# One-core sparse spike FFN: batch 0's chain moved into the wait for batch 1's totals, the idle row made ahead of the last table chunks, and all stores but one held behind the second gather of w1 rows

## The reference, cut to what matters

```python
# x: (2, 2048, 512) float32, cond: (2, 512), w1: (512, 2048), w2: (2048, 512)
rates = relu(x) * 0.001
c = cond[:, None, :] + cumsum(rates, axis=1)          # along the 2048 tokens
fl = floor(c)
prev = concatenate([floor(cond)[:, None, :], fl[:, :-1, :]], axis=1)
spikes = (fl - prev) / 0.001
h = relu(spikes @ w1 + b1)
out = x + h @ w2 + b2
```

## Time and profile before

| what | us |
|---|---|
| median of three runs | 105.44 (105.04 to 106.31) |
| the profiled execution's own time | 105.28 |
| its span in the profile | 103.4 |
| last store issued by SP | 81.32 |
| first scatter of batch 1 on POOL | 91.21 |
| last scatter (general rows) on POOL | 98.68 |
| last matmul of the general FFN ends | 96.37 |

### The profile page before, as it was taken

How to read it: one execution, slowest core, us unless ns; L and a number is a source line. 1 busy time by engine, 2 the same in 40 slices (tenths; PEclk the granted TensorE clock), 3 DMA queues, 4 the chain that set the end, 5 groups by cost and what they waited for, 6 DMA issues and landing times.

```text
span 103.4 us, 1080 instructions
## 1 busy us (share of the span) xinstructions
PE 90.7 (88%) x325; PEld 46.2 (45%) x325; DVE 67.9 (66%) x152; ACT 36.5 (35%) x66; POOL 34.3 (33%) x39
## 2 busy tenths in 40 slices
PE   5999999999999999999999699992699999999200
PEld 5934444444644444644132235440656666665000
DVE  3448999989599999485848758998999500012200
ACT  2886515415281540569940000002136222222000
POOL 6220000000068600017604894000000678568840
PEclk9999999999999999999999999999759999999995
DMA  2999999999999999940000069989999999968770
GB/s 78 287 375 396 421 420 412 406 406 410 415 407 411 378 401 398 411 184 6 10 3 0 0 222 412 282 257 409 418 437 421 424 437 361 205 157 87 102 130 30
DMA packets 8203, 29.55 MB, mean 286 GB/s; under 512 B 1639, under 2 KB 1767, under 8 KB 6914
## 3 DMA queue, kind: packets, MB, share of 16 engines
q1 hardware_dynamic: 6192, 25.43, 61.9%
q0 software_dynamic: 1856, 4.00, 18.0%
q10 hardware_dynamic: 146, 0.01, 0.1%
HBM read 19.48 MB, written 10.75 MB: 292 GB/s over the span
## 4 chain that ended last, share of the span: by engine, by line
PE 44%; DVE 25%; DMA 9%; ACT 7%; issue 4%; POOL 4%; POOLq 2%; DVEq 0%
PE ps_table L886 37%; DVE x_sb L748 15%; DMA out<-x_sb 9%; POOL out L379 4%; PE ps_small L1017 4%; ACT w_sb L456 3%; ACT w_sb L455 2%; POOLq L55 2%; PE ps_turn L923 2%; DVE place_hot L693 1%; PE ps_idle L912 1%; DVE under L611 1%; DVE place_slot L700 1%; ACT block_sum L465 1%; ACT idle_base L486 0%
## 5 line engine op out<-in xcount | busy, mean ns | idle before, releaser
L886 PE MATMUL ps_table<-w_sb 128*128 128x512 f32 x128 | 58.5, 603 | 0.0
L886 PEld LDWEIGHTS ps_table<-w_sb 128*128 128x128 f32 x128 | 23.4, 192 | 24.2 <-issue 23.1
L368 POOL DMA_INDIRECT rates<-in_x_turned,sixteen_at x8 | 9.8, 1225 | 35.5 <-DVE sixteen_at L615 33.7
L379 POOL DMA_INDIRECT out<-w_sb,to_single x8 | 12.5, 1565 | 20.0 <-DMA out<-x_sb 18.2
L455 ACT ACTIVATE w_sb<-w_sb,b_col 128x512 f32<-128x512 f32 (+2 forms) x19 | 12.2, 643 | 17.0 <-DMA w_sb<-in_w_pairs 16.9
L601 DVE SCALAR_TENSOR_TENSOR total_two<-x_sb,total_two 128x1024 f32<-128x1024 f32 x14 | 17.1, 1225 | 0.8 <-DMA x_sb<-in_x 0.4
L991 PE MATMUL ps_table<-w_sb 128*128 128x512 f32 x32 | 17.2, 626 | 0.0
L748 DVE TENSOR_TENSOR x_sb<-x_sb,ps_idle 128x2048 f32<-128x2048 f32 x7 | 15.6, 2281 | 0.1
L456 ACT ACTIVATE w_sb<-w_sb,minus_relu_b 128x512 f32<-128x512 f32 (+2 forms) x19 | 12.3, 649 | 0.6
L983 PEld LDWEIGHTS ps_turn<-place_slot,w_sb 128*128 128x128 f32 x32 | 5.2, 209 | 7.6 <-issue 7.0
L559 DVE SCALAR_TENSOR_TENSOR idle_part<-w_sb,relu_b,idle_part 128x512 f32<-128x512 f32 x9 | 6.8, 753 | 1.7 <-DMA w_sb<-in_w_pairs 1.5
(11 more groups left out here) (152 smaller groups left out, 61.7 us busy)
## 6 DMA issues: line engine op xcount, KB each, us to landing
x_sb<-in_x SPq DMA_DIRECT2D x16, 512.0 KB, 14.5
out<-x_sb SPq DMA_DIRECT2D x8, 1024.0 KB, 8.1
w_sb<-in_w_pairs SPq DMA_DIRECT2D x15, 512.0 KB, 15.6
w_sb<-in_w_pairs SPq DMA_DIRECT2D x2, 256.0 KB, 2.9
b_row<-in_b SPq DMA_DIRECT2D x1, 256.0 KB, 15.5
rates<-in_x_turned,sixteen_at POOLq DMA_INDIRECT x8, 4.3
out<-w_sb,to_single POOLq DMA_INDIRECT x8, 5.7
w_sb<-in_w,w_at POOLq DMA_INDIRECT x2, 8.0
```

What stands on the lines that cost most here:

```text
L368: pool.indirect_dma_start(out=rates[:, col, :], out_offset=None, in_=x_sixteen, in_offset=bass.IndirectOffsetOnAxis(ap=sixteen_at[:, col:c ...
L379: pool.indirect_dma_start(out=out_rows, out_offset=bass.IndirectOffsetOnAxis(ap=to, axis=0), in_=row, in_offset=None, bounds_check=last_ro ...
L886: last = pe.matmul(ps_table[c][:, :], table_hidden[:, m, c * P:(c + 1) * P], w2_sb[:, m, :], start=(m == 0), stop=(m == FC - 1))
```

## The change

What it does:

- PE takes one more chunk of the idle row and DVE one less (`BY_HAND` 9 becomes 8).
- SP's second store (batch 0, tokens 4 to 7) first waits for `w1_got[1]`, the landing of the second gather of w1 rows. The six stores behind it on SP wait with it.
- POOL issues the first gather of w1 rows ahead of its adds, no longer waits for `places_ready` before them, and adds 8 tokens of batch 0 instead of 4: seven between the two gathers, one behind the second. DVE adds the other 8 tokens of batch 0: one behind `find_tokens(1)`, one behind `number_general(1)`, two and four behind `list_places(1)`.
- DVE runs `find_tokens(0)` ahead of `find_blocks(1)`, and the rest of batch 0's chain up to `list_places(0)` ahead of `find_tokens(1)`.
- PE turns batch 0's blocks behind chunk 6, and takes batch 0's steps and the strips earlier among the table's parts.
- ACT copies batch 0's turned blocks behind chunk 10, and the two idle copies and batch 1's turned blocks ahead of chunks 14 and 15.

```diff
--- before.py
+++ after.py
@@ -37,7 +37,7 @@
     WQ = 4
     STRIP = 32
     STRIPS = P // STRIP
-    BY_HAND = 9
+    BY_HAND = 8
     WARM = 8
     FAR = 4.0 * ROWS
     NEVER = 1.0e30
@@ -326,6 +326,8 @@
                 sp.dma_start(out_blk[b, :, piece(q), :], x_sb[b][:, piece(q), :]).then_inc(idle_stored[b], 16)
 
             for b, q in ((0, 0), (0, 1), (0, 2), (0, 3), (1, 0), (1, 1), (1, 2), (1, 3)):
+                if (b, q) == (0, 1):
+                    sp.wait_ge(w1_got[B - 1], 16)
                 store_idle(b, q)
             for b in range(B):
                 sp.wait_ge(idle_stored[b], 16 * XQ)
@@ -389,12 +391,11 @@
 
             get_sixteens(0)
             get_sixteens(1)
+            get_w1(0)
             pool.wait_ge(idle_copied, 1)
-            pool.wait_ge(places_ready, 1)
-            add_idle(0, 0, 2)
-            get_w1(0)
-            add_idle(0, 2, 4)
+            add_idle(0, 0, 7)
             get_w1(1)
+            add_idle(0, 7, 8)
             pool.wait_ge(singles_listed, 1)
             for b in range(B):
                 if b == 1:
@@ -480,13 +481,14 @@
                     copy_sums(0)
                 if m == 11:
                     copy_sums(1)
-                if m == 14:
+                if m == 10:
                     copy_blocks(0)
-            act.wait_ge(strips_summed, 1)
-            act.activation(idle_base[:, :], ps_idle[:, :], ACT.Copy).then_inc(strips_copied, 1)
-            act.wait_ge(idle_summed, 1)
-            act.activation(idle_row[:, :], ps_idle[:, :], ACT.Copy).then_inc(idle_copied, 1)
-            copy_blocks(1)
+                if m == 13:
+                    act.wait_ge(strips_summed, 1)
+                    act.activation(idle_base[:, :], ps_idle[:, :], ACT.Copy).then_inc(strips_copied, 1)
+                    copy_blocks(1)
+                    act.wait_ge(idle_summed, 1)
+                    act.activation(idle_row[:, :], ps_idle[:, :], ACT.Copy).then_inc(idle_copied, 1)
 
             def relu_hidden(m, summed, count, ready):
                 act.wait_ge(summed, count)
@@ -748,6 +750,8 @@
                 last = dve.tensor_tensor(tokens, tokens, along(ps_idle[:, :], end - begin), ALU.add)
                 if end % TQ == 0:
                     last.then_inc(idle_added[b][end // TQ - 1], 1)
+                else:
+                    chain(last)
 
             first_columns()
             idle_by_hand(0)
@@ -771,30 +775,30 @@
             block_totals(1, 3, 5)
             find_sums(0)
             block_totals(1, 5, 6)
-            idle_by_hand(8)
             block_totals(1, 6, XH)
+            find_tokens(0)
             find_blocks(1)
-            find_tokens(0)
+            find_general(0)
             pick_blocks(1)
-            find_general(0)
+            number_general(0)
             find_sums(1)
-            number_general(0)
-            find_odd()
             find_slots(0)
             count_members(0)
+            find_odd()
             place_members(0)
+            list_places(0)
             find_tokens(1)
-            list_places(0)
+            add_idle(0, 8, 9)
             find_general(1)
             number_general(1)
+            add_idle(0, 9, 10)
             find_slots(1)
             count_members(1)
             place_members(1)
             list_places(1)
-            add_idle(0, 4, 8)
+            add_idle(0, 10, 12)
+            add_idle(0, 12, 16)
             copy_rows()
-            add_idle(0, 8, 12)
-            add_idle(0, 12, 16)
             list_singles()
             list_general()
             for q in range(XQ):
@@ -1022,39 +1026,40 @@
             for m in range(2, 6):
                 table_chunk(m)
             sum_totals(0)
-            for m in range(6, 9):
+            table_chunk(6)
+            turn_blocks(0)
+            for m in range(7, 10):
                 table_chunk(m)
-            table_chunk(9)
             table_part(10, 0, 3)
             sum_totals(1)
+            count_tokens(0)
+            add_strips(0, STRIPS)
             table_part(10, 3, DC)
-            table_part(11, 0, 3)
-            turn_blocks(0)
-            table_part(11, 3, DC)
-            count_tokens(0)
-            add_strips(0, FC - BY_HAND + 1)
+            table_part(11, 0, 1)
             count_before(0)
-            table_part(12, 0, 1)
-            join_strips()
+            add_strips(STRIPS, FC - BY_HAND + 1)
             give_back(0)
             turn_blocks(1)
-            table_part(12, 1, 2)
+            table_part(11, 1, 3)
+            join_strips()
+            table_part(11, 3, DC)
             count_members(0)
-            table_part(12, 2, 3)
+            table_part(12, 0, 1)
             sum_places(0)
-            table_part(12, 3, DC)
+            table_part(12, 1, DC)
+            table_part(13, 0, 2)
             count_tokens(1)
-            table_part(13, 0, 1)
+            table_part(13, 2, 3)
             count_before(1)
-            table_part(13, 1, 2)
+            table_part(13, 3, DC)
             give_back(1)
-            table_part(13, 2, 3)
+            table_part(14, 0, 1)
             count_members(1)
-            table_part(13, 3, DC)
+            table_part(14, 1, 2)
             sum_places(1)
-            table_part(14, 0, 1)
+            table_part(14, 2, 3)
             sum_rows()
-            table_part(14, 1, DC)
+            table_part(14, 3, DC)
             table_chunk(15)
 
             pe.wait_ge(rows_copied, 1)
```

## The result

The changed kernel takes 107.01 us (median of 18 runs, 106.43 to 107.98) against 105.72 us of the kernel before (18 runs): **ratio 1.0164, 95% interval 1.0134 to 1.0195.** That is 1.6% slower, clear of no change, but under the 2% that the prediction counts as the same. The prediction was 104.7 us, 0.7% faster. Its range (103.4 to 107.2 us) held the time, but by luck: its upper end was made for a gather of 7.8 us, and the gather took 6.0. The time moved the other way. The profiled execution of the changed kernel took 107.07 us, with a span of 105.3 us.

A forecast was written before the change was run, and what follows sets the result against it. Bound: DMA engines' store backlog, setting batch 1's last store. Gather lands 70.2, last store 90.2, first scatter 90.5, span end 12.2 us later at 102.7; plus 1.88 around the span and 0.16 to the median, 104.7 us (range 103.4 to 107.2).

The forecast's parts named there:

- a gather of 7.8 us: Second gather of w1 rows, halfway to the slow one: 2.5 us more, setting the range's upper end of 107.2 us.
- The chain of batch 0: DVE and PE steps up to batch 0's row list: `w1_at[0]` at 54.3 instead of 57.68, 3.4 us earlier.
- POOL: POOL's adds start at 55.5, seven take 9.1 us; second gather issued at 64.9, 1.4 us later than before.
- The second gather's landing: Second gather of w1 rows on quiet engines: takes 5.3 us, lands at 70.2, 3 us earlier than before.
- The lower end, 4.9: Shortest second-gather time considered, from the first gather's data being through 4.9 us after its issue.
- the window of 69 to 72.5: Second gather's landing times that the main forecast covered, with a chance of 0.81, slowed adds included.
- The stores: Seven stores without a gap from 70.3: first takes 5.1 us, others 2.46 apart, last lands at 90.2 against 90.94.
- What the stores lose by the later start they get back: Stores behind the hold: without the gather's slowdown and sharing, the last lands at 90.2 against 90.94.
- That PE's earlier start is worth nothing: PE's general FFN: starts at 70.2 instead of 73.35, ends near 93, needed by 98; these 3 us gain nothing.
- The second gather stays slow: Rival, second gather: still takes 9.7 us, lands at 74.6, all stores wait, 109.1 us; chance 0.08.
- POOL's adds are slowed: Rival, POOL's seven adds beside DVE's chain: each loses 0.3 us, giving 106.8 us; counted inside the forecast's 0.81.
- The rule that the prediction cites, on two inputs from SBUF: For slowed POOL adds: a DVE instruction with two SBUF inputs excludes a GpSimd instruction reading SBUF for its whole length.

The follow-up runs named there:

- run 4: Changed kernel with batch 0's scatters also waiting for batch 1's stores, so no scatter runs beside a store: 113.94 us in one run.
- runs 5: Changed kernel without the hold, adds dealt out anew between POOL and DVE so the second store is ready earlier: 107.48 us, ratio 1.0173 to the kernel before.
- run 8: Run 6's kernel with two more adds on POOL ahead of the second gather and two fewer on DVE: 105.3 us, ratio 0.994 to the kernel before.
- run 9: Run 6's kernel with the first store held until batch 1's list of w1 rows is made: 107.65 us, ratio 1.0207 to the kernel before.
- run 6: Changed kernel without the hold and with POOL's and DVE's adds dealt out as in the kernel before: 104.35 us, ratio 0.9883 to the kernel before.
- run 7: Run 5's kernel with the hold put back, the second store waiting for the second gather's landing: 107.15 us, ratio 1.0142 to the kernel before.

## Why the prediction was wrong, step by step

- **The chain of batch 0.** Right: `w1_at[0]` at 54.65 (54.3 said). DVE still idled 1.20 us ahead of batch 1's blocks with `find_tokens(0)` in the gap.
- **POOL.** Mechanism right, 0.9 us short. The adds start at 56.04 (55.5) and the seven end at 65.50, 9.46 us for 9.1. The gather is issued at 65.76 (64.9).
- **The second gather's landing.** Mis-sized: 6.00 us with quiet engines, where I took 5.3 and gave 6.3 as the worse end. The lower end, 4.9, counted to the last byte and not to the landing: in the changed kernel the engines are still (share 0.02) from 71 on and the landing is at 71.76. The first gather of the changed kernel took 6.5 just as quiet. With the 0.9 above, the landing is at 71.76 instead of 70.2. By the Trainium skill, "DMA: Bandwidth & Descriptors", section "Anatomy of one DMA — SWDGE (gpsimd) path", an estimate by the page's fit is 4.4 us; the measurement decides, and no quiet gather of these kernels took under 5.7. At 71.76, inside the window of 69 to 72.5 that the prediction gave itself, its own sum gives 106.3 us, which is already slower than before.
- **The stores. This is the step that failed.** The prediction said "What the stores lose by the later start they get back". They did not. I set an undisturbed run of stores in the changed kernel (5.1 + 6 x 2.46) against a measured landing of the kernel before (81.32 + 9.62), which already contained the scatters' share: its last two stores land 2.65 and 4.1 us behind their predecessors. The 5.1 us was not a price on quiet engines either, since the first gather was landing then. In the changed kernel the first of the seven took 3.9 instead of 5.1 (1.2 gained) but the six behind it 17.1 instead of 14.8 (2.3 lost); run 4 puts 2.1 of that on batch 0's scatters, which ran beside the last two stores. So the stores are 1.1 us longer than priced and the gather's landing 1.5 later: 92.8 instead of 90.2. Either one was enough to turn the forecast gain of 0.7 us into a loss. That 2.6 closes the account: first scatter at 93.08 instead of 90.5, 12.2 behind it 105.3 instead of 102.7.
- **That PE's earlier start is worth nothing.** Right in the changed kernel, where PE ends 7 us before it is needed. But it is a bound at little distance: in runs 5, 8 and 9 POOL waited for the same row (3.5, 2.1 and 1.0 us).
- **Which part costs.** I had the hold free, the adds at 1.4 us in the gather's issue, and the chain worth nothing by itself. The runs give: moved chain alone 0.988; with the adds dealt out anew 1.002; with the hold 1.016. So the chain was worth 1.2%, and the two others each took about 1.4% away (each of these is uncertain by some 0.5%).
- **The rivals.** "The second gather stays slow" did not happen, since it ran alone. "POOL's adds are slowed" did not either (1.27 us each). DVE was the one held up: `place_slot` took 1.36 us against 282 ns undisturbed. It started within 0.02 us of POOL's seventh add (64.23 to 65.50) and ended 0.07 us behind it. By the Trainium skill, "SBUF — State Buffer", section "Who interferes with whom", a VectorE instruction in a two-port mode and a GpSimd instruction lock each other out, and the one that comes second waits for the whole instruction; the trace agrees in that `place_slot` ended with the add, and does not show its mode. The rule that the prediction cites, on two inputs from SBUF, does not reach `place_slot`, which reads `name_f` from SBUF and `ps_turn` from PSUM. PE's `sum_rows` was 0.6 us late by it, without effect on the end.

What stays open: why a store that leaves just ahead of a gather slows it that much (11 us against 6), more than its own 2.46 us of the engines. By the Trainium skill, "DMA: Bandwidth & Descriptors", section "Queues, rings and completion order", an engine takes turns between queues that have work; that agrees with the table in direction, and no run here splits the rest. That the moved chain gains through the distance between first store and second gather is shown only from one side, by run 9: run 6's first gather and first store also leave 0.9 us earlier than before (57.7 and 61.4), and its first gather has landed before the second leaves. No run held these fixed.

## What to carry to other kernels

A wait that keeps bulk transfers out of a critical gather's way saves the gather and costs the time in which the engines then stand idle, on both sides of the gather; where the bulk sets the end, spacing the issues some 2 to 4 us apart gave the gather nearly all of that (6.4 to 6.6 us) without a wait. A forecast must price both kernels in the same way: if a transfer of the kernel before is taken as measured, with all that runs beside it, the same transfer of the changed kernel can't be taken at its undisturbed price. And when two chains end within some 2 us of each other, as stores and PE do here, ask of each gain on the one what it does to the other.

## What the runs showed of the hardware

- A gather of 128 rows of 8 KB took 5.7 to 6.5 us with no other transfer near it, and in the changed kernel it was slow at first even then: 142 GB/s at a DMA share of 0.82 in its first 1.5 us, 334 GB/s later. The 197 GB/s of before were thus not the stores' doing alone.
- The same gather, with the first gather landed, took 9.0 us with a store issued 0.6 us behind it (run 8) and 11.1 with one 0.2 us ahead of it and the next 2.2 us behind (run 9). With no store near but the first gather under way for 3.1 us it took 7.9 (run 7, one trace).
- Scatters with addition that are issued while stores are queued take from the last of them: 2.1 us for four scatters (run 4 against the changed kernel).
